# A gated delta-rule attention and mixture-of-experts layer: each expert's earliest tokens kept as running lists through attention, and five of eight shared groups placed behind the experts

## The chip, the cores and the metric

The kernel runs on one core of a Trainium2 chip. Its engines are TensorE (PE), VectorE (DVE), ScalarE (ACT), GpSimd (POOL) and SyncE (SP), each with an instruction queue of its own that runs in order. The metric is the device time of one execution in microseconds (us). The profile is of one execution; the times before are three other ones.

## The reference, cut to what matters

```python
B, S, D = 2, 2048, 256; H, DK, DV = 16, 128, 128; SEG = 64      # attention
def step(carry, seg):                     # 32 segments in order, per head and batch
    mem, z = carry; qq, kk, vv = seg
    att_dot = softmax(where(causal, qq @ kk.T / scale, -inf)) @ vv
    att_mem = sigma_q @ mem / (sigma_q @ z)
    delta = vv - sigma_k @ mem / (sigma_k @ z)
    mem_new = mem + sigma_k.T @ delta
    z_new = z + sigma_k.sum(tokens)
    att = beta * att_mem + (1 - beta) * att_dot
    return (mem_new, z_new), att @ Wo
x1 = x + attention(layernorm(x)); h = layernorm(x1)

E, K, G, TG, CAP = 32, 4, 4, 2, 64        # experts, 4 of 32 per token
topk_idx, topk_w = gate(h)                # sigmoid, best 2 of 4 groups, best 4 experts
pos = cumsum(one_hot(topk_idx)) - 1       # place of a token in its expert's queue
keep = pos < CAP                          # an expert takes its 64 earliest tokens
out = sum_k topk_w[k] * expert(topk_idx[k], h) where keep
shared = silu(h @ shared_gate) * (h @ shared_up) @ shared_down
return x1 + out + shared
```

Of the 4096 tokens (2 batches of 2048) each expert keeps only the 64 that come first, so all but the earliest picks of an expert are dropped.

## The kernel before

**Attention.** The program walks over 16 blocks of 128 tokens (of both batches at once), and in each block over 8 pairs of heads, the steps g = 0 to 7 (`body(blk, first, last)`, written once for every engine and unrolled). Step n = 8 blk + g has two segments (seg 0 and 1). TensorE's row of work in a step: numerators of segment 0 (L1354), projections for the next step (L1305), update of segment 0 (L1364), numerators of segment 1, projections, update of segment 1, `attend` (L1381), scores of the next step (L1328), then the numerators of the next step. `numerators` waits for the semaphore `mem_ready`, which VectorE's `state(n, g, seg)` gives after it has subtracted the update from the memory (two instructions at L902, of `chain_k` and `chain_q`). VectorE's row in a step ends: delta of segment 1 (L883 to L892), whatever of the layer norms and the gate stands in that step, `sigma_q(n + 1)` (L868), `state(n, g, 1)` (L902), and then the next step's `attended` (L911), mask (L1074) and maximum (L1079).

The rest of the layer rides along one block late: output projection in g = 0 (`project_out`, L1410), residual in g = 1 (L919), layer norm in g = 1 to 3, gate in g = 5 to 7. GpSimd does the elementwise work between (L474, L480, L489, L498).

**Routing.** `picks(blk)` (L1007) turns a block's picks into one descending number for each token (`N` minus its place; 0 if not picked), 32 experts on 32 partitions by 256 tokens, and SyncE writes it to the DRAM tensor `picks`. After the last block GpSimd writes that block's part itself, reads the whole tensor back as `vq` (128 partitions, four quarters of the tokens, by 1024), and `top8` (L1056 MAX8, L1057 MATCH_REPLACE8) takes the eight greatest eight times over; the four lists of 64 are moved side by side (`cm`, 32 x 256) and `top8` runs eight times again. The result gives the token numbers for the gathers of GpSimd (L573).

**Shared expert.** 8 groups (`NTG`) of 2 blocks. A group is `shared_up` (two halves fc, each a gate and an up product, L1462), ScalarE's silu (L744), VectorE's `shared_mul` (L1044), `shared_down` (L1481) and `shared_add` into `acc` (L1050). `shared_mul(g, fc)` waits until `shared_down(g - 1)` is over, since both use the buffer `sh`. `FRONT = 7` groups stand ahead of the experts, one behind them. The first half of group 0 stands inside the last attention step, where there is nothing to project, and waits there for the shared weights to land.

**Experts.** 16 pairs (`NP`): gather rows, transpose (`columns`, L1498), up (L1510), down (L1526), merge (L1538 to L1541), and GpSimd scatters the rows with an accumulate to the DRAM tensor `y` (L586). When all 16 scatters have landed, SyncE loads `y` in four parts (L431), VectorE adds each to `acc` (`sum_add`, L1276) and SyncE stores it (L436).

## Time and profile before

| | us |
|---|---|
| median of three executions | 1823.45 (1822.89 to 1825.72) |
| the profiled execution: its time | 1825.59 |
| the profiled execution: its span, first to last instruction | 1823.7 |
| TensorE busy in the span | 1728.6 (95%), 17990 matmuls |
| VectorE busy | 1208.0 (66%) |
| ScalarE, GpSimd busy | 805.4 (44%), 916.7 (50%) |

The profiled execution's time is 1.9 us over its span and 2.1 us over the median. A busy share is a mean over very different stages: the attention loop fills nearly 1640 us of the span, the rest of the layer the last 184 us. In rows of the timeline the columns are start, duration, engine, line, operation, written and read tiles, shapes and count, and in square brackets the idle time of the engine before it with what ended it.

### The profile page before, as it was taken

The numbers are of one execution on the slowest core, as the hardware profiler recorded it, in microseconds if no ns is written. First come the engines' busy times: TensorE is split into PE (matmuls) and PEld (weight loads), VectorE is DVE, ScalarE is ACT, GpSimd is POOL, SyncE is SP. The second block draws the span as 40 slices with busy tenths as digits, with TensorE's granted clock in tenths as the row PEclk, the third lists the DMA queues.
The fourth block names the chain that finished last, engine by engine and source line by source line (L and its number), as shares of the span: only waits on it lengthen the run. The fifth ranks groups of instructions, "written<-read, shape, count | busy, mean of one in ns | idle before, by whom it ended". The sixth has DMA issues, their size and how long they took to land. (4 is left out here: it accounts for less than half of the span.)

```text
span 1823.7 us, 45885 instructions
## 1 busy us (share of the span) xinstructions
PE 1728.6 (95%) x17990; PEld 1473.8 (81%) x17990; DVE 1208.0 (66%) x3996; ACT 805.4 (44%) x1936; POOL 916.7 (50%) x830
## 2 busy tenths in 40 slices
PE   6999999999999999999999999999999999989893
PEld 5788888888888888888888888888888888866451
DVE  6766757575767767575767677675767675663852
ACT  3544535353535445353535354453535354541040
POOL 3655646464646546464646455454646464530162
PEclk8999999999999999999999999999999999999997
DMA  4200000100000000001000000000010000046747
GB/s 152 70 22 25 15 19 8 32 8 25 15 15 25 15 25 15 19 8 32 8 22 18 15 25 15 25 15 19 8 32 8 15 25 9 25 148 188 207 80 202
DMA packets 83190, 75.23 MB, mean 41 GB/s; under 512 B 20992, under 2 KB 73808, under 8 KB 82720
## 3 DMA queue, kind: packets, MB, share of 16 engines
q1 hardware_dynamic: 79264, 65.89, 11.9%
q0 software_dynamic: 3680, 6.40, 1.9%
q8 instruction: 144, 2.36, 0.5%
q14 instruction: 70, 0.57, 0.1%
q10 hardware_dynamic: 32, 0.01, 0.0%
HBM read 47.78 MB, written 24.47 MB: 40 GB/s over the span
## 5 line engine op out<-in xcount | busy, mean ns | idle before, releaser
L489 POOL TENSOR_TENSOR step_place<-step_place 128x512 f32<-128x512 f32 x128 | 169.7, 1326 | 243.5 <-ACT step_place L645 243.5
L659 ACT ACTIVATE step_place<-chain_q,step_place 128x128 f32<-128x128 f32 x512 | 159.9, 366 | 275.2 <-DVE step_place L886 274.9
L902 DVE TENSOR_TENSOR step_place<-step_place,chain_k 128x258 f32<-128x258 f32 x256 | 107.7, 421 | 260.7 <-PE chain_q L1364 260.6
L525 POOL TENSOR_TENSOR step_place<-step_place 128x256 f32<-128x256 f32 x128 | 78.8, 615 | 313.5 <-DVE step_place L1079 313.5
L1410 PE MATMUL bank_o<-step_place 128*128 128x256 f32 x1024 | 226.0, 379 | 0.0
L480 POOL TENSOR_SCALAR step_place<-step_place 128x512 f32<-128x512 f32 x128 | 191.0, 1492 | 44.0 <-ACT step_place L639 43.9
L1410 PEld LDWEIGHTS bank_o<-step_place 128*128 128x128 f32 x1024 | 192.3, 190 | 25.4 <-issue 0.5
L474 POOL TENSOR_SCALAR step_place<-step_place 128x512 f32<-128x512 f32 x128 | 190.3, 1486 | 0.3 <-POOL step_place L498 0.3
L1354 PE MATMUL chain_k<-step_place 128*64 128x129 f32 x2048 | 166.0, 282 | 20.3 <-DVE step_place L902 20.2
L1364 PE MATMUL chain_k<-step_place 64*128 64x129 f32 x1024 | 181.4, 297 | 1.8 <-ACT step_place L659 1.1
L1364 PE MATMUL chain_q<-step_place 64*128 64x129 f32 x1024 | 181.6, 297 | 0.0
L1364 PEld LDWEIGHTS chain_k<-step_place 64*128 64x128 f32 x1024 | 132.4, 186 | 44.8 <-issue 42.3
L498 POOL TENSOR_TENSOR step_place<-step_place 128x512 f32<-128x512 f32 x128 | 164.6, 1286 | 0.0
L892 DVE SCALAR_TENSOR_TENSOR step_place<-chain_k,step_place 128x128 f32<-128x128 f32 x512 | 154.4, 342 | 6.1 <-DVE step_place L883 0.8
L1354 PE MATMUL chain_q<-step_place 128*64 128x129 f32 x2048 | 158.1, 273 | 0.0
L532 POOL TENSOR_TENSOR step_place<-step_place 128x256 f32<-128x256 f32 x128 | 78.5, 613 | 153.6 <-DVE step_place L1087 153.6
L652 ACT ACTIVATE step_place<-bank_k 128x512 f32<-128x512 f32 x128 | 76.7, 599 | 160.4 <-PE chain_q L1364 155.6
L1354 PEld LDWEIGHTS chain_k<-step_place 128*64 128x64 f32 x2048 | 109.2, 137 | 43.2 <-issue 29.3
L627 ACT ACTIVATE step_place<-bank_q 128x512 f32<-128x512 f32 x128 | 76.5, 598 | 136.0 <-PE bank_q L1305 136.0
L1364 PEld LDWEIGHTS chain_q<-step_place 64*128 64x128 f32 x1024 | 132.5, 186 | 0.0
L1354 PEld LDWEIGHTS chain_q<-step_place 128*64 128x64 f32 x2048 | 122.8, 136 | 0.0
L1305 PE MATMUL bank_k<-xt_hi,w_hi 128*128 128x256 f32 x512 | 116.6, 309 | 1.1 <-DVE xt_lo L860 1.1
(201 smaller groups left out, 4342.1 us busy)
## 6 DMA issues: line engine op xcount, KB each, us to landing
expert_place<-in_L_ffn_w_dram SPq DMA_DIRECT2D x24, 512.0 KB, 7.8
expert_sums<-zero SPq DMA_DIRECT2D x16, 272.0 KB, 5.1
expert_rows<-w_in SPq DMA_DIRECT2D x15, 288.0 KB, 2.2
step_place<-in_L_attn_x_dram SPq DMA_DIRECT2D x16, 256.0 KB, 3.0
x_res<-in_L_attn_x_dram SPq DMA_DIRECT2D x16, 256.0 KB, 3.2
x_rows<-w_in SPq DMA_DIRECT2D x16, 256.0 KB, 2.0
x_normed_t<-x1t SPq DMA_DIRECT2D x16, 256.0 KB, 2.0
shared_place<-x_normed_t SPq DMA_DIRECT2D x8, 512.0 KB, 8.2
```

The source lines that it names most:

```text
L474: nc.gpsimd.tensor_scalar(ex_q[:, :], ex_q[:, :], 1.0, None, ALU.min).then_inc(s["q_min"], 1)
L480: nc.gpsimd.tensor_scalar(ex_k[:, :], ex_k[:, :], 1.0, None, ALU.min).then_inc(s["k_min"], 1)
L489: nc.gpsimd.tensor_tensor(vb[:, :, :, :].rearrange("p s j d -> p s (j d)"), val[:, :, :, :].rearrange("p s j d -> p s (j d)"), rows.unsque ...
L498: nc.gpsimd.tensor_tensor(vo[:, :, :, :], val[:, :, :, :], vb[:, :, :, :], ALU.subtract).then_inc(s["vo_ready"], 1)
L525: nc.gpsimd.tensor_tensor(sm[:, :, :], sm[:, :, :], smx[:, :].unsqueeze(2).to_broadcast([128, T, SEG]), ALU.subtract).then_inc(s["s_shifte ...
L659: ins = nc.scalar.activation(am[:, par, seg, j, :], chain_q[:, j * ZC:j * ZC + DK], ACT.Copy, scale=rdq[:, seg, j:j + 1])
L892: ins = nc.vector.scalar_tensor_tensor(out=dl[seg][:, j, 0:DK], in0=chain_k[:, j * ZC:j * ZC + DK], scalar=rdk[:, seg, j:j + 1], in1=vb[:, ...
L902: ins = nc.vector.tensor_tensor(m, m, (chain_k, chain_q)[b][:, 0:HG * ZC].rearrange("p (j z) -> p j z", j=HG), ALU.subtract)
L1305: ins = mm(out, w[:, g, m, c, col], x[:, c, :, :].rearrange("p s t -> p (s t)"), start=i == 0, stop=i == len(parts) - 1)
L1354: ins = mm(out[ROWS[half], j * ZC:(j + 1) * ZC], sig[:, j, seg, b, :], mem[:, HG * g + j, b, :], start=True, stop=True)
L1364: ins = mm((chain_k, chain_q)[b][:, j * ZC:(j + 1) * ZC], ksig[ROWS[b], j, seg, :], dl[seg][ROWS[b], j, :], start=True, stop=True)
L1410: ins = mm(bank_o[:, b * D:(b + 1) * D], att[:, b * PIECES + i, :], wo[:, i, :], start=(i == 0 and b == 0), stop=(i == PIECES - 1), skip_g ...
```

## The change

- The lists of the earliest tokens are kept while attention runs. A buffer `earliest[blk % 2]` has one partition for each batch and expert (64), with 64 places for the list so far and 128 for the block's new picks. `picks` writes the 128 new numbers, and in every step g of blocks 2 to 15 one round (`earliest_of`: a MAX8 and a MATCH_REPLACE8 over 64 x 192) stands between `sigma_q` and `state`. The last block's eight rounds stand behind the loop. The DRAM tensor `picks`, `vq`, `cm` and their transfers are gone; after the last gate 8 rounds run over 32 x 384.
- `FRONT = 3`: three shared groups stand ahead of the experts and five behind. The half of group 0 that stood in the last step goes behind the last output projection.
- The loads of `x1t` for groups 4 to 7 wait until the scatters have left their places. The four `sum_add` stand between the shared groups behind the experts, and the last two blocks are stored one by one.

```diff
-STEP_PLACE = 23808
+STEP_PLACE = 23760
-    FRONT = 7
+    FRONT = 3
-    XSLOT = [0, 1, 2, 3, 4, 0, 1, 4]
+    XSLOT = [0, 1, 2, 4, 0, 1, 2, 3]
...
+        for g in range(4, NTG):
+            sp.wait_ge(s2["added"], 64 * (g - 3))
+            load_columns(g)
...
-        for k in range(NK):
+        for k in range(NK - 1):
             sp.wait_ge(s2["y_added"], k + 1)
             store(k * YB, (k + 1) * YB)
+        sp.wait_ge(s2["y_added"], NK)
+        store((NK - 1) * YB, NBLK - TG)
+        for k in range(NBLK - TG, NBLK):
+            sp.wait_ge(s2["acc_ready"], k + 1)
+            store(k, k + 1)
...
-        for q in range(QUARTERS):
-            pool.dma_start(vq[q * E:(q + 1) * E, :], scratch["picks"][:, q * QUART:(q + 1) * QUART]
-                           ).then_inc(s2["vq_arrived"], 16)
...
         def picks(blk):
...
+            nc.vector.tensor_tensor(earliest[blk % 2][:, CAP:CAP + BLK], bank_o[0:B * E, 0:BLK],
+                                    desc[:, :], ALU.mult).then_inc(s["pickv_ready"], 1)
             dve.wait_ge(s["pickv_ready"], blk + 1)
+            nc.vector.tensor_scalar_add(desc[:, :], desc[:, :], -float(BLK)
                                         ).then_inc(s["desc_ready"], 1)
+        def earliest_of(blk, r):
+
+            link = link_on(dve, s["list_step"], 2 * ROUNDS * (blk - 1) + 2 * r + 1)
+            have, kept = earliest[blk % 2], earliest[(blk + 1) % 2][:, 8 * r:8 * r + 8]
+            link(nc.vector.max(kept, have[:, :]))
+            link(nc.vector.match_replace(out=have[:, :], in_to_replace=kept, in_values=have[:, :],
+                                         imm_value=-1.0))
...
                     sigma_q(n + 1, (g + 1) % 2)
+                if blk > 1:
+                    earliest_of(blk - 1, g)
                 if first and g + 2 < NG:
                     split_lo(g + 2)
                 state(n, g, 1)
...
+        for r in range(ROUNDS):
+            earliest_of(NBLK - 1, r)
...
         for r in range(ROUNDS):
+            top8(sel, pool_last[:, :, :].rearrange("p b c -> p (b c)"), r)
+            if r == 0:
+                shared_mul(1, 0)
+            if r == 2:
+                shared_mul(1, 1)
+            if r in (3, 4):
+                shared_add(0, r - 3)
+            if r == 6:
+                shared_mul(2, 0)
...
+        for g in range(FRONT, NTG):
+            shared_mul(g, 0)
+            if g > FRONT:
+                for k in range(TG):
+                    shared_add(g - 1, k)
+            if g == NTG - 2:
+                sum_add(0)
+            if g == NTG - 1:
+                sum_add(2)
+            shared_mul(g, 1)
+            if g == NTG - 2:
+                sum_add(1)
+            if g == NTG - 1:
+                sum_add(3)
+        dve.wait_ge(s2["y_added"], NK)
```

The instructions that move, as they stand in the two programs. First VectorE, step g = 1 of the last block, from the statistics of the residual to the next step's first addition. Before:

```order
L818 BN_STATS st_x<-w_in 128x6 x2
L821 BN_AGGR mv_x<-st_x 128x2 x2
L823 TENSOR_SCALAR v_x<-mv_x 128x2
L824 TENSOR_SCALAR a_x<-v_x 128x2
L826 TENSOR_SCALAR rs_x<-a_x 128x2
L868 SCALAR_TENSOR_TENSOR step_place<-bank_q,step_place 128x512
L902 TENSOR_TENSOR step_place<-step_place,chain_k 128x2x129
L902 TENSOR_TENSOR step_place<-step_place,chain_q 128x2x129
L911 TENSOR_TENSOR step_place<-step_place,bank_a 128x256
```

After:

```order
L807 TENSOR_SCALAR v_x<-mv_x 128x2
L808 TENSOR_SCALAR a_x<-v_x 128x2
L810 TENSOR_SCALAR rs_x<-a_x 128x2
L852 SCALAR_TENSOR_TENSOR step_place<-bank_q,step_place 128x512
L1006 MAX earliest<-w_in 64x8
L1007 MATCH_REPLACE w_in<-earliest,w_in 64x192
L886 TENSOR_TENSOR step_place<-step_place,chain_k 128x2x129
L886 TENSOR_TENSOR step_place<-step_place,chain_q 128x2x129
L895 TENSOR_TENSOR step_place<-step_place,bank_a 128x256
```

A round of the list now stands in the queue between `sigma_q` and `state`. Next TensorE, from the last `attend` (L1381, after L1382) to the rows behind the last output projection (L1410, after L1411). Before:

```order
L1381 MATMUL bank_a<-step_place 64x128 x2
L1381 MATMUL bank_v<-step_place 64x128 x2
L1462 MATMUL chain_k<-shared_place 128x512 x2
L1391 MATMUL bank_a<-step_place 128x2x16x4 x4
L1462 MATMUL chain_q<-shared_place 128x512 x2
L1410 MATMUL bank_o<-step_place 128x256 x32
```

After:

```order
L1382 MATMUL bank_a<-step_place 64x128 x2
L1382 MATMUL bank_v<-step_place 64x128 x2
L1392 MATMUL bank_a<-step_place 128x2x16x4 x4
L1411 MATMUL bank_o<-step_place 128x256 x32
L1461 MATMUL bank_q<-shared_place 128x512 x2
L1461 MATMUL bank_k<-shared_place 128x512 x2
L1461 MATMUL chain_k<-shared_place 128x512 x2
L1421 MATMUL bank_o<-ident,w_in 128x128 x4
L1429 MATMUL bank_o<-gwt,x1t 128x32 x4
```

No shared product is left ahead of the output projection, and none between the transposes of the normed rows and the logits. Last, the end of TensorE's program. Before, from the last merge on:

```order
L1538 MATMUL chain_q<-shared_place 128x256
L1539 MATMUL chain_q<-shared_place 128x256
L1541 MATMUL bank_s<-shared_place 128x256
L1462 MATMUL bank_q<-shared_place 128x512 x2
L1462 MATMUL bank_k<-shared_place 128x512 x2
L1462 MATMUL chain_k<-shared_place 128x512 x2
L1462 MATMUL chain_q<-shared_place 128x512 x2
L1481 MATMUL bank_s<-shared_place 128x256 x4
L1481 MATMUL bank_v<-shared_place 128x256 x4
```

After, the last two groups of the five:

```order
L1461 MATMUL chain_k<-shared_place 128x512 x2
L1461 MATMUL chain_q<-shared_place 128x512 x2
L1461 MATMUL bank_q<-shared_place 128x512 x2
L1461 MATMUL bank_k<-shared_place 128x512 x2
L1480 MATMUL bank_s<-shared_place 128x256 x4
L1480 MATMUL bank_v<-shared_place 128x256 x4
L1461 MATMUL chain_k<-shared_place 128x512 x2
L1461 MATMUL chain_q<-shared_place 128x512 x2
L1480 MATMUL bank_s<-shared_place 128x256 x4
L1480 MATMUL bank_v<-shared_place 128x256 x4
```

A group's down product stands between the two halves of the next group's up product, and the last one stands alone.

## Rows read from the trace of the kernel before

**Rows 1.** Timeline, VectorE and TensorE at the ends of block 14's steps 0 to 3

```profile
1452.18 0.42 DVE L902 TENSOR_TENSOR step_place<-step_place,chain_k 128x258 f32<-128x258 f32 x1 [7.92 <-PE chain_q L1364]
...
1462.65 0.41 DVE L902 TENSOR_TENSOR step_place<-step_place,chain_k 128x258 f32<-128x258 f32 x1
...
1472.94 0.42 DVE L902 TENSOR_TENSOR step_place<-step_place,chain_k 128x258 f32<-128x258 f32 x1 [0.32 <-PE chain_q L1364]
1473.28 0.42 DVE L902 TENSOR_TENSOR step_place<-step_place,chain_q 128x258 f32<-128x258 f32 x1
...
1473.94 0.61 PE L1354 MATMUL chain_k<-step_place 128*64 128x129 f32 x8
...
1483.74 0.42 DVE L902 TENSOR_TENSOR step_place<-step_place,chain_k 128x258 f32<-128x258 f32 x1 [0.74 <-PE chain_q L1364]
```

**Rows 2.** Timeline, the same two engines at the ends of steps 5 to 7

```profile
1505.63 0.42 DVE L902 TENSOR_TENSOR step_place<-step_place,chain_k 128x258 f32<-128x258 f32 x1 [0.44 <-PE chain_q L1364]
...
1516.91 0.42 DVE L902 TENSOR_TENSOR step_place<-step_place,chain_q 128x258 f32<-128x258 f32 x1
...
1517.76 0.61 PE L1354 MATMUL chain_k<-step_place 128*64 128x129 f32 x8
...
1529.01 0.40 DVE L902 TENSOR_TENSOR step_place<-step_place,chain_q 128x258 f32<-128x258 f32 x1
...
1529.56 0.66 PE L1354 MATMUL chain_k<-step_place 128*64 128x129 f32 x8 [1.07 <-DVE step_place L902]
```

**Rows 3.** Timeline, VectorE: starts of two neighbouring rounds, of 1024 and of 256

```profile
1686.00 1.23 DVE L1056 MAX8 shared_place<-shared_place 128x8 f32<-128x1024 f32 x1 [8.21 <-DMA shared_place<-picks]
...
1688.58 1.23 DVE L1056 MAX8 shared_place<-shared_place 128x8 f32<-128x1024 f32 x1
...
1719.08 0.42 DVE L1056 MAX8 shared_place<-shared_place 32x8 f32<-32x256 f32 x1
...
1720.04 0.42 DVE L1056 MAX8 shared_place<-shared_place 32x8 f32<-32x256 f32 x1
```

**Rows 4.** Timeline, VectorE in step 6 of block 14, while GpSimd is busy

```profile
1511.77 0.15 DVE L963 MATCH_REPLACE8 grp<-glist,gsx 128x10 f32<-128x10 f32 x1
...
1512.09 1.28 DVE L966 TENSOR_SCALAR gm<-grp 128x8 f32<-128x8 f32 x1
```

**Rows 5.** Timeline, TensorE from the last step to the last output projection

```profile
1623.57 3.75 PE L1462 MATMUL bank_q<-shared_place 128*128 128x512 f32 x4 [3.37 <-DMA shared_place<-x_normed_t]
...
1630.29 0.37 PE L1364 MATMUL chain_k<-step_place 64*128 64x129 f32 x1
...
1640.36 13.98 PE L1410 MATMUL bank_o<-step_place 128*128 128x256 f32 x64
```

**Rows 6.** Timeline, VectorE: residual of the last block; the multiply behind its picks

```profile
1654.38 0.69 DVE L919 TENSOR_TENSOR w_in<-bank_o,x_res 128x512 f32<-128x512 f32 x1 [13.05 <-PE bank_o L1410]
...
1670.86 0.66 DVE L1044 TENSOR_TENSOR shared_place<-shared_place,chain_q 128x512 f32<-128x512 f32 x1
```

**Rows 7.** Timeline, TensorE: down products two groups apart, first expert columns, shared group behind

```profile
1701.67 1.89 PE L1481 MATMUL bank_v<-shared_place 128*128 128x256 f32 x8
...
1722.31 1.89 PE L1481 MATMUL bank_v<-shared_place 128*128 128x256 f32 x8
...
1733.01 0.38 PE L1498 MATMUL bank_o<-ident,shared_place 128*128 128x128 f32 x2
...
1782.74 1.98 PE L1462 MATMUL bank_q<-shared_place 128*128 128x512 f32 x4 [0.47 <-ACT shared_place L786]
```

**Rows 8.** DMA issues: count, KB each, median us from issue to landing

```profile
x_rows<-w_in SPq DMA_DIRECT2D x16, 256.0 KB, 2.0
...
shared_place<-picks POOLq DMA_DIRECT2D x4, 128.0 KB, 6.7
...
shared_place<-expert_rows,shared_place POOLq DMA_INDIRECT x16, 3.0
```

**Rows 9.** Busy time in a stretch; the number behind POOL is the granted clock

```profile
1620.00:1640.00 20.00, 14.25 (x80) 7.57 (x77) 7.57 (x31) 5.94 (x15) 2.45 (x3) 0.83 0.76 266
```

More of the change, by code:

```diff
@@ L216, in layer @@
     wsum = sb("wsum", [128, 3, B])
[L217 removed]
+    desc = sb("desc", [B * E, BLK])
     small = sil[:, :, :].rearrange("p a c -> p (a c)")
@@ L412, in _ @@
         sp.wait_ge(s["wo_mm"], NBLK)
-        for i in range(NB // 2):
-            load_batch(i)
-        sp.wait_ge(s2["u_mm"], 2 * FC)
-        load_columns(6)
-        for i in range(NB // 2, NB):
+        for i in range(NB):
             load_batch(i)
@@ L466, in _ @@
                                     channel_multiplier=1).then_inc(s["const_ready"], 1)
-        nc.gpsimd.iota(desc[:, :, :], pattern=[[-S, B], [-1, BLK]], base=N, channel_multiplier=0,
-                       allow_small_or_imprecise_dtypes=True).then_inc(s["desc_ready"], 1)
+        pool.wait_ge(s["const_ready"], 3)
+        for b in range(B):
+            nc.gpsimd.iota(desc[b * E:(b + 1) * E, :], pattern=[[-1, BLK]], base=N - b * S,
+                           channel_multiplier=0, allow_small_or_imprecise_dtypes=True
+                           ).then_inc(s["desc_ready"], 1)
         def cap_queries(n):
@@ L754, in _ @@
         ins.then_inc(s2["ident_kept"], 1)
-        shared_silu(1, 0)
+        shared_silu(0, 0)
+        shared_silu(0, 1)
         side_x1t(NBLK)
         logits_exp(NBLK)
-        shared_silu(1, 1)
-        for g in range(2, FRONT):
+        for g in range(1, FRONT):
             for fc in range(FC):
@@ L1135, in _ @@
         attended(NT - 1, (NG - 1) % 2)
-        for fc in range(FC):
-            shared_mul(0, fc)
+        for r in range(ROUNDS):
+            earliest_of(NBLK - 1, r)
+        for b in range(B):
+            ins = nc.vector.tensor_copy(pool_last[:, b, 0:CAP],
+                                        earliest[NBLK % 2][b * E:(b + 1) * E, 0:CAP])
+        ins.then_inc(s["lists_kept"], 1)
         residual(NBLK)
@@ L1141, in _ @@
         x1_apply(NBLK)
-        dve.wait_ge(acc_arrived[0], 16)
-        for k in range(TG):
-            shared_add(0, k)
-        shared_mul(1, 0)
+        shared_mul(0, 0)
         gate_scores(NBLK)
@@ L1190, in _ @@
         for k in range(TG):
-            shared_add(5, k)
-        for fc in range(FC):
-            shared_mul(6, fc)
+            shared_add(1, k)
+        shared_mul(2, 1)
         def weights(q):
@@ L1276, in sum_add @@
             nc.vector.tensor_tensor(a, a, y, ALU.add).then_inc(s2["y_added"], 1)
-        for fc in range(FC):
-            shared_mul(NTG - 1, fc)
+        for g in range(FRONT, NTG):
[13 more added lines that the diff above has]
+        dve.wait_ge(s2["y_added"], NK)
         for k in range(TG):
             shared_add(NTG - 1, k)
-        for k in range(NK):
-            sum_add(k)
     @block.tensor
@@ L1433, in pick_transposes @@
             pe.wait_ge(s["gate_step"], GATE_STEPS * (blk - 1) + PICK_STEP)
-            for b in range(B):
-                ins = nc.tensor.transpose(bank_o[0:E, b * BLK:(b + 1) * BLK], pick[:, b, :],
-                                          ident[:, :])
-            ins.then_inc(s["pickt_mm"], 1)
+            nc.tensor.transpose(bank_o[0:B * E, 0:BLK], pick[:, :, :].rearrange("p b e -> p (b e)"),
+                                ident[:, :]).then_inc(s["pickt_mm"], 1)
         pe.wait_ge(s["ident_ready"], 6)
@@ L1599, in _ @@
         pe.wait_ge(s["mem_ready"], 2 * NT)
-        shared_half(0, 1, 0)
         attended_transposes(NT - 1, (NG - 1) % 2)
-        shared_half(0, 1, 1)
         pe.wait_ge(s["pickv_ready"], NBLK)
         project_out(0, PIECES, NT)
-        shared_down(0)
-        pe.wait_ge(xt_arrived[1], 16)
-        shared_half(1, 0, 0)
-        x1_transposes(NBLK)
-        shared_half(1, 0, 1)
-        logits(NBLK)
-        shared_up(1, 1)
+        pe.wait_ge(s2["shared_arrived"], 48)
+        shared_up(0, 0)
+        shared_half(0, 1, 0)
+        x1_transposes(NBLK)
+        logits(NBLK)
+        shared_half(0, 1, 1)
+        shared_up(1, 0)
+        pick_transposes(NBLK)
+        shared_up(1, 1)
+        shared_down(0)
         shared_up(2, 0)
-        pick_transposes(NBLK)
-        shared_half(2, 1, 0)
         shared_down(1)
-        shared_half(2, 1, 1)
-        for g in range(3, FRONT):
-            shared_up(g, 0)
-            shared_down(g - 1)
-            if g == FRONT - 1:
-                pe.wait_ge(s["pickv_ready"], NBLK + 1)
-                pair_tokens()
-            shared_up(g, 1)
-        shared_down(FRONT - 1)
+        pe.wait_ge(s["pickv_ready"], NBLK + 1)
+        pair_tokens()
+        shared_up(2, 1)
+        shared_down(2)
         columns(0)
@@ L1638, in _ @@
         pe.wait_ge(s2["yo_ready"], NP)
-        shared_up(NTG - 1, 0)
-        shared_up(NTG - 1, 1)
+        for g in range(FRONT, NTG):
+            shared_up(g, 0)
+            if g > FRONT:
+                shared_down(g - 1)
+            shared_up(g, 1)
         shared_down(NTG - 1)
```

108 lines of the change are left out of this document (33 added, 75 removed).

## The prediction

> **What bounds the kernel now.** I read the timeline first, at the ends of the steps of one attention block, because the change puts two VectorE instructions into every one of them. Attention is a loop of 100.6 us per block (step 0 of block 14 ends its wait at 1452.18 [rows 1]; the pattern repeats to 0.1 us in blocks 2 to 14). TensorE is nearly gapless there, so anything that makes it wait is paid in full, 14 times. The question at each step's end is who comes last: VectorE with `state` (L902), which TensorE's next numerators (L1354) wait for, or TensorE with its own queue. The bracket behind an L902 row is VectorE's idle time, that is, its cover. In step 0 it is 7.92 us, in step 1 none, in step 2 0.32, in step 3 0.74 [rows 1], in step 5 0.44, in steps 6 and 7 none [rows 2]. There is a second, smaller cover: the time from the end of `state` to TensorE's start. Where TensorE really waits (step 7, bracket 1.07) it is 1529.56 - 1529.41 = 0.15 [rows 2]. In step 2 it is 1473.94 - 1473.70 = 0.24 [rows 1], so 0.09 is slack; in step 6 it is 1517.76 - 1517.33 = 0.43 [rows 2], so 0.28 is slack.
>
> Then the timeline behind the loop. TensorE waits 3.37 us for the shared weights and does a shared half before it can go on with the last step [rows 5]. Later VectorE waits 8.21 us for `picks` to come back from DRAM [rows 3], and then makes lists for 38 us, while shared groups fill TensorE. At the end only scatters, loads of `y`, adds and stores are left.
>
> **Part 1: a list round in each step.** The trace has no round of 192, but two sizes beside it, with their waits in the start-to-start time: 2.58 us for 1024 (1686.00 to 1688.58) and 0.96 for 256 (1719.08 to 1720.04) [rows 3]. The slope is 1.62 / 768 = 0.0021 us per element, so 192 takes 0.96 - 64 x 0.0021 = 0.83 us. Bounds: not over 0.96, the row of 256, and not under some 0.55, which the fixed part would be if the line were steeper near its foot. I take 0.83, from the nearest row. GpSimd is busy beside it, and some VectorE instructions wait for it: a TENSOR_SCALAR of 8 elements takes 1.28 us, while a MATCH_REPLACE8 just before it takes 0.15 [rows 4]. So the match form does not wait, and I add nothing. The Trainium skill, SBUF — State Buffer, Who interferes with whom, says that a VectorE instruction with at most one SBUF input outside the two-port modes does not contend with GpSimd; by that rule, the trace agrees.
>
> What of 0.83 reaches TensorE, step by step: step 0 nothing; step 1 0.83; step 2 0.83 - 0.32 - 0.09 = 0.42; steps 3 and 4 nothing (0.74 idle and more slack; step 4 has more idle time still); step 5 0.83 - 0.44 - 0.09 = 0.30; step 6 0.83 - 0.28 = 0.55; step 7 0.83, since there VectorE is last already. A delay is not made up later, since TensorE has no idle time to give back, and it does not grow, since VectorE waits for TensorE in the middle of each step. Sum 2.93, or 5x - 1.22 for a round of x. For 13 blocks 38.0 us. In the last block (steps 1, 2, 5 and 6, the last without slack) 4x - 0.94 = 2.4. Together **+40 us**. The cheaper picks (64 x 128 in place of 32 x 256, one transpose fewer) are worth perhaps 0.1 us a block, in step 7 alone; I leave them out. The eight rounds behind the loop (6.6 us) lie under the output projection, 13.98 us [rows 5], for which VectorE only waits (13.05) [rows 6]. Without that cover they would cost their 6.6.
>
> **Part 2: the end of attention.** TensorE has its numerators done at 1623.57 - 3.37 = 1620.20 and starts the update at 1630.29 [rows 5]. With no load to wait for, the update needs only VectorE's delta, some 1.0 us: 9.1 us gained. VectorE takes back about 0.9 of it on the way to the last `attended` (a round, and its softmax sum comes last). Ahead of the output projection at 1640.36 [rows 5] two shared halves of 1.7 us go, and about 1.4 us of waits for VectorE and ScalarE that they covered stay open: 2.0 gained. Together **-10.2 us**.
>
> **Part 3: from the residual to the experts.** Before: 1654.38 [rows 6] to 1733.01 [rows 7], 78.6 us. A group costs TensorE half of 1722.31 - 1701.67, 10.3 us [rows 7], and four of them leave this stretch, but what bounds it then is VectorE's chain. Counted from the residual: the multiply behind the picks ended at 17.1 (1670.86 + 0.66 [rows 6]); logits come 0.6 earlier and the picks are 0.5 shorter, so 16.0. A round of 384 takes 0.96 + 128 x 0.0021 = 1.23. The first ends at 17.2. Then `shared_mul(1, 0)` stands in VectorE's queue, and it waits for `shared_down(0)`, which TensorE can begin only when the multiply at 16.0 has let it finish the second half of group 1 (17.7) and ends 3.45 later, at 21.1. Seven rounds (8.6) and five VectorE shared operations at 0.6 lead to 32.8, the three index steps, the transposes and the copies to 34.2. TensorE has run dry meanwhile, and then does the second half of group 2 (3.4), waits for its multiply (0.9) and does the down product (3.45): the first expert columns stand at 41.8. So **-36.8 us**.
>
> The gathers now start while the expert weights are still streaming: SyncE starts them 7 us behind the residual and needs over 40 us, as before. Small transfers of GpSimd took 3.0 us to land behind that stream (gathers) and 6.7 in the midst of it (`picks`) [rows 8]. The first gather would land at 35.3 + 6.7 = 42.0, just in time. But gathers 2 and on are queued on GpSimd behind the wait for the token list's store, and VectorE's second `hidden` behind the 1 MB token load. I put **+4 us** on it, between 0 (all lands in 3.0) and 9 (nothing lands before the weights are through).
>
> **Part 4: the end.** Before, the experts give way to the last group at 1782.74 [rows 7] and the span ends at 1823.7. Scatters, loads and adds of `y` (some 30 us) are now covered by five groups: 1782.74 + 5 x 10.3 = 1834.3; about 1.5 for the last multiply, which stands behind an add of `y`; 0.7 for the last add; 0.9 to issue two stores and 2.0 to land (a store of 256 KB [rows 8]): 1839.4, **+15.7 us**. If the `y` loads were late, they would have 20 us to spare.
>
> **Part 5: the clock.** Between 1620 and 1640 TensorE had 0.83 of its clock [rows 9]: 0.17 x 20 / 0.5 = 6.8 us at 1.2 in place of 2.4 GHz, after short stops and the one of 3.37. After the change two stretches are as thin: the last step, and the wait for the index. A fall costs up to half its length where TensorE is busy, so 0 to 3.4 each: **+2 us**.
>
> **Sum.** 40.4 - 10.2 - 36.8 + 4 + 15.7 + 2 = +15.1. Span 1823.7 + 15.1 = 1838.8; the profiled execution was 1.9 over its span and 2.1 over the median, so the forecast is **1838.5 us**, 0.8% slower. The tail gains 25 us and the loop loses 40.
>
> **Rivals.** (a) *The round is cheap or finds cover: faster.* Place: between L868 and L902 in steps 1, 2, 5, 6, 7. The loop costs 69x - 16.8 in all. It breaks even with the tail at 25 us, x = 0.61, and the kernel is over 0.2% faster under x = 0.56. At x = 0.4 the time would be 1811 (the terms of steps 2 and 5 end at nothing). For it: the MATCH_REPLACE8 of 10 elements takes 0.15 [rows 4], so the fixed part is small. Against it: the two sizes of rows 3 lie on one line, and 192 is close to 256. (b) *Partly covered*: a time of 1820 to 1827, if steps 2, 5 and 6 give more slack than their rows (that is 17 us of the 40). (c) *The longer stops pull down the clock.* The stop in step 7 grows from 1.07 [rows 2] to 1.9 us. The clock stayed at 2.4 GHz through all stops of 1.07, and fell after the thin stretch with the one of 3.37 [rows 5, 9]. If it falls in a third of the blocks, at 2 to 3.4 us each, that is 8 to 15 us: 1847 to 1854. The Trainium skill, TensorE: Matmul & The Clock Gate, HAM oscillation, tells of loops that throttle in every pass because of stops in them; by that rule it could be all 14 blocks, near 1880. (d) *The experts do not start early*, since their gathers and the token list land only with the last weights: 5 us more, 1844, and with two cold stretches 1848.
>
> **How the numbers follow.** Forecast 0.60 (own range 1829 to 1846), (a) 0.12, (b) 0.08, (c) 0.14, (d) 0.06. A measurement of this kernel can tell about 0.2%, 3.6 us, from no change. Slower by more: 0.80; within: 0.08; faster: 0.12. The range of 1822 to 1852 leaves out (a) and the upper part of (c).
>
> **What would show it.** In the trace after: MAX8 and MATCH_REPLACE8 of 64 x 192, 0.83 us from start to start of their neighbours; a block period of 103.5 us in place of 100.6; waits of TensorE for L902's successor in steps 1, 2, 5, 6 of 0.8, 0.4, 0.3, 0.5 us and 1.9 in step 7; output projection to first columns 37 us shorter; TensorE busy to some 4 us before the end. A period under 102.4 with the tail as computed would make the prediction wrong in sign, and a granted clock under 0.98 between the second and fourteenth block would make it (c).

## The result, and the profile of the changed kernel

The changed kernel takes 1857.22 us (median of four executions, 1855.78 to 1858.58) against 1823.69 of the kernel before beside it: ratio 1.0182, 95% interval 1.0164 to 1.0200. The forecast was 1838.5 us with a range of 1822 to 1852. The direction was right, the loss is 33.5 us in place of 15, and the time lies outside the range. The profiled execution of the changed kernel took 1855.78 us with a span of 1854.0.

Where the 30.3 us of span went, from the same marks in both traces (in us; a negative number is a gain):

| stretch | before | after | difference | forecast |
|---|---|---|---|---|
| start to step 0 of block 2 | 221.7 | 222.25 | +0.6 | 0 |
| blocks 2 to 14 | 1307.9 | 1355.6 | +47.8 | +38.0 |
| block 15, its steps 0 to 6 | 89.5 | 93.8 | +4.3 | +2.4 |
| last step to last output projection | 21.26 | 12.01 | -9.25 | -10.2 |
| projection to residual | 14.02 | 15.82 | +1.8 | 0 |
| residual to first expert columns | 78.63 | 43.90 | -34.7 | -36.8 |
| columns to the first group behind the experts | 49.73 | 53.40 | +3.7 | +4 |
| from there to the end | 40.96 | 57.2 | +16.2 | +15.7 |

The clock's +2 of the forecast belongs to the last five lines together. These came to -22.3 where -25.3 was forecast; the first three came to +52.6 where +40.4 was forecast.

First the marks and waits of TensorE. The timeline's columns are those of the groups of before. Kernel before, TensorE, the two marks not shown yet (step 0 of block 2, last step of block 15):

```profile
221.70 0.55 PE L1354 MATMUL chain_k<-step_place 128*64 128x129 f32 x6 [1.08 <-DVE step_place L902]
...
1619.10 0.66 PE L1354 MATMUL chain_k<-step_place 128*64 128x129 f32 x8 [1.37 <-DVE step_place L902]
```

Changed kernel, TensorE's numerators (L1355): the mark at block 2, behind steps 1, 6 and 7 of block 3, behind step 7 of block 4, and the mark at block 15. They answer to the TensorE rows of [rows 1, 2]:

```profile
222.25 0.55 PE L1355 MATMUL chain_k<-step_place 128*64 128x129 f32 x6 [1.33 <-DVE step_place L886]
...
361.22 0.33 PE L1355 MATMUL chain_k<-step_place 128*64 128x129 f32 x2 [0.67 <-DVE step_place L886]
...
416.72 0.44 PE L1355 MATMUL chain_k<-step_place 128*64 128x129 f32 x4 [0.37 <-DVE step_place L886]
...
429.40 0.33 PE L1355 MATMUL chain_k<-step_place 128*64 128x129 f32 x2 [2.00 <-DVE step_place L886]
...
532.93 0.66 PE L1355 MATMUL chain_k<-step_place 128*64 128x129 f32 x8 [2.01 <-DVE step_place L886]
...
1577.89 0.66 PE L1355 MATMUL chain_k<-step_place 128*64 128x129 f32 x4 [2.52 <-DVE step_place L886]
```

The cause of the waits stands on VectorE, between `sigma_q` (L852) and `state` (L886), at the end of block 4:

```profile
530.61 0.67 DVE L852 SCALAR_TENSOR_TENSOR step_place<-bank_q,step_place 128x512 f32<-128x512 f32 x1
531.21 0.34 DVE L1006 MAX8 w_in<-earliest 64x8 f32<-64x192 f32 x1
531.58 0.08 DVE L1007 MATCH_VALUE_LOAD earliest<-w_in,earliest 64x8 f32 x1
531.66 0.33 DVE L1007 MATCH_REPLACE8 earliest<-w_in,earliest 64x192 f32<-64x192 f32 x1
532.03 0.42 DVE L886 TENSOR_TENSOR step_place<-step_place,chain_k 128x258 f32<-128x258 f32 x1
```

A round costs 532.03 - 531.21 = 0.82 us, as forecast, and the block period without anything else is 103.5 to 103.6, as forecast. Every second block or so is longer. Busy time in stretches of the changed kernel (the number behind POOL's is the clock granted to TensorE as a share of 2.4 GHz): blocks 4 and 5, then the 3.4 us around the stop that ends block 4 and the 3.4 us behind it:

```profile
429.40:532.90 103.50, 99.70 (x1089) 87.32 (x1089) 74.59 (x261) 47.40 (x115) 53.65 (x48) 1.00 0.06 17
532.90:638.00 105.10, 101.25 (x1090) 88.76 (x1090) 74.68 (x261) 47.36 (x115) 53.61 (x48) 0.98 0.06 17
...
530.10:533.50 3.40, 1.39 (x34) 1.15 (x28) 3.33 (x10) 0.31 (x1) 0.51 (x1) 1.00 0.55 164
533.50:536.90 3.40, 3.40 (x22) 3.06 (x18) 2.16 (x8) 0.93 (x3) 1.17 (x2) 0.50 0.03 7
```

Behind the stop of 2.01 us TensorE has 1.2 GHz for 3.4 us; step 0 of block 5 takes 25.72 us in place of 24.22, so the fall costs 1.5 us. The trace has seven of these falls, at the starts of blocks 5, 6, 8, 10, 11, 13 and 15 (the last behind the stop of 2.52 us): 10.5 us. The kernel before had none between 41.8 and 1622.

Now the part behind the loop. Changed kernel, TensorE:

```profile
1671.69 0.66 PE L1355 MATMUL chain_k<-step_place 128*64 128x129 f32 x8 [2.56 <-DVE step_place L886]
...
1683.70 15.78 PE L1411 MATMUL bank_o<-step_place 128*128 128x256 f32 x64 [0.90 <-ACT step_place L660]
...
1726.73 1.96 PE L1480 MATMUL bank_s<-shared_place 128*128 128x256 f32 x8 [2.41 <-DVE shared_place L1046]
...
1733.41 0.29 PE L1487 MATMUL bank_o<-ident,shared_place 32*64 32x16 f32 x4 [2.96 <-DVE shared_place L1176]
1733.63 2.48 PE L1461 MATMUL chain_k<-shared_place 128*128 128x512 f32 x4
1735.90 3.13 PE L1461 MATMUL chain_q<-shared_place 128*128 128x512 f32 x4
...
1743.42 0.38 PE L1497 MATMUL bank_o<-ident,shared_place 128*128 128x128 f32 x2
...
1748.64 0.69 PE L1497 MATMUL bank_o<-ident,shared_place 128*128 128x128 f32 x2 [2.79 <-DMA shared_place<-expert_rows,shared_place]
...
1796.82 1.98 PE L1461 MATMUL bank_q<-shared_place 128*128 128x512 f32 x4 [0.47 <-ACT shared_place L770]
```

and VectorE: the residual, the multiply of group 1 between the rounds over 384 places, the index:

```profile
1699.52 0.69 DVE L903 TENSOR_TENSOR w_in<-bank_o,x_res 128x512 f32<-128x512 f32 x1 [10.99 <-PE bank_o L1411]
...
1721.02 0.69 DVE L1040 TENSOR_TENSOR shared_place<-shared_place,bank_k 128x512 f32<-128x512 f32 x1 [4.53 <-PE bank_v L1480]
...
1733.81 0.17 DVE L1178 CAST shared_place<-bank_o 128x16 uint32<-128x16 f32 x1 [0.54 <-PE bank_o L1487]
```

The output projection is stretched from 13.98 us [rows 5] to 15.78, and the two matmul groups at 1733.63 and 1735.90 take 2.48 and 3.13 us where their neighbours take 1.88: the granted clock was at 1.2 GHz from 1680.4 to 1687.2 and from 1735.0 to 1738.4.

### The profile page after: what moved, and what is told of

It is laid out like the page before. It is cut to its first block, busy times and chain, and to the rows that moved or that the text cites. A ratio compares the mean times of both kernels' runs of the same rounds, so it can differ in the third digit from the quotient of the medians.

```text
span 1854.0 us, 46269 instructions
## 1 busy us (share of the span) xinstructions
PE 1750.4 (94%) x17974; PEld 1488.9 (80%) x17974; DVE 1269.1 (68%) x4335; ACT 804.5 (43%) x1936; POOL 912.5 (49%) x822
## 4 chain that ended last, share of the span: by engine, by line
PE 69%; DVE 21%; issue 4%; ACT 2%; POOL 2%; DMA 1%; SPq 0%; DVEq 0%; POOLq 0%; ACTq 0%
PE bank_o L1411 12%; PE bank_k L1306 10%; PE bank_q L1306 9%; PE chain_k L1355 7%; PE chain_k L1365 5%; PE chain_q L1355 5%; PE bank_v L1316 5%; PE bank_a L1392 3%; DVE step_place L886 3%; PE bank_s L1329 2%; DVE step_place L852 2%; PE bank_a L1382 2%; DVE step_place L876 2%; PE bank_s L1400 1%; PE bank_k L1338 1%
## 5 line engine op out<-in xcount | busy, mean ns | idle before, releaser
L886 DVE TENSOR_TENSOR step_place<-step_place,chain_k 128x258 f32<-128x258 f32 x256 | 108.4, 423 | 223.0 <-PE chain_q L1365 218.7
L1411 PE MATMUL bank_o<-step_place 128*128 128x256 f32 x1024 | 227.8, 381 | 0.9 <-ACT step_place L660 0.9
L1355 PE MATMUL chain_k<-step_place 128*64 128x129 f32 x2048 | 169.2, 284 | 51.2 <-DVE step_place L886 50.7
L1411 PEld LDWEIGHTS bank_o<-step_place 128*128 128x128 f32 x1024 | 193.5, 191 | 26.6 <-issue 1.3
L1355 PEld LDWEIGHTS chain_k<-step_place 128*64 128x64 f32 x2048 | 111.1, 137 | 80.3 <-issue 65.0
L1355 PE MATMUL chain_q<-step_place 128*64 128x129 f32 x2048 | 161.5, 275 | 0.0
L1355 PEld LDWEIGHTS chain_q<-step_place 128*64 128x64 f32 x2048 | 125.7, 137 | 0.0
```

The costliest lines, as they stand in the source:

```text
L886: ins = nc.vector.tensor_tensor(m, m, (chain_k, chain_q)[b][:, 0:HG * ZC].rearrange("p (j z) -> p j z", j=HG), ALU.subtract)
L1355: ins = mm(out[ROWS[half], j * ZC:(j + 1) * ZC], sig[:, j, seg, b, :], mem[:, HG * g + j, b, :], start=True, stop=True)
L1411: ins = mm(bank_o[:, b * D:(b + 1) * D], att[:, b * PIECES + i, :], wo[:, i, :], start=(i == 0 and b == 0), stop=(i == PIECES - 1), skip_g ...
```

## Experiments

The loop costs more than its rounds by the clock, in the profile of one execution. The theory: **one long stop** of TensorE, at the end of step 7, brings the clock down. The rivals: the sum of the stops in a block does it, or something else of the change (its transfers, its picks). The first four kernels move rounds between step 0, where VectorE has 7.92 us of idle time [rows 1], and the others. All their edits are the same line with another condition:

```diff
                 if blk > 1:
-                    earliest_of(blk - 1, g)
+                    for r in range(ROUNDS):
+                        if 0 == g:
+                            earliest_of(blk - 1, r)
```

with `(7 if r > 6 else 0) == g` for one round in step 7, `(7 if r > 5 else 0) == g` for two, and `max(r - 1, 0) == g` for none in step 7.

### All rounds in step 0

> The changed kernel with all eight rounds of a block's list in step 0, where VectorE had 7.9 us of idle time before the second state; eight rounds take 8 x 0.82 = 6.6 us. If the rounds cost only what TensorE waits for, and the falls of the clock come only from the longer stop at the end of step 7 (2.0 us in place of 1.07), then the block period goes back from 103.55 to 100.6 us and no fall is left between the second and the last block: span 1854.0 - 38.4 (13 blocks) - 3.2 (last two) - 10.5 (seven falls of 1.5) = 1802, time about 1804. That is then the change's tail alone, 22 us under the kernel before. If the falls have another cause in the changed kernel (its new DMA traffic, its smaller picks), they stay: about 1814. If step 0 has less cover than its idle time says (the round's instructions wait for something there), the period ends between 101 and 103 us: 1808 to 1835.

Measured: 1801.92 us, 1.2% under the kernel before (ratio 0.9880, 0.9864 to 0.9897). The block period is 100.57 us and no fall is left in the loop. VectorE in step 0 of block 3, the end of the last round and the `state` that follows, and the stretch of the loop:

```profile
343.50 0.33 DVE L1007 MATCH_REPLACE8 w_in<-earliest,w_in 64x192 f32<-64x192 f32 x1
345.29 0.42 DVE L886 TENSOR_TENSOR step_place<-step_place,chain_k 128x258 f32<-128x258 f32 x1 [1.45 <-PE chain_q L1367]
```

```profile
42.00:1620.00 1578.00, 1546.18 (x17089) 1359.26 (x17088) 1161.42 (x3977) 752.04 (x1813) 849.73 (x755) 1.00 0.07 20
```

After eight rounds VectorE still waits 1.45 us for TensorE. The 112 rounds of the loop, with which (falls included) the changed kernel's loop took 52 us more, cost nothing here, and the falls went with the stops. This kernel is the change without the loop's cost: the rest of it is worth 22.7 us in the medians.

### One round in step 7

> Seven rounds in step 0 (covered), the eighth in step 7 as in the changed kernel. The only stop that grows is the one at the end of step 7, to 2.0 us; those of steps 1, 2, 5 and 6 are gone. Theory 'the single long stop': the clock still falls behind it in about half of the blocks: period 101.5 without a fall, loop +13 us and 7 falls at 1.5 us, 1804 + 13 + 10.5 = 1827. Rival 'the sum of the stops in a block' (3.2 us in the changed kernel, 2.0 here): no or hardly any fall, 1817.

Measured: 1828.60 us (ratio 1.0023, 1.0013 to 1.0033). Blocks 2 and 3:

```profile
222.40:323.90 101.50, 98.91 (x1091) 87.03 (x1092) 75.21 (x261) 47.49 (x115) 53.65 (x48) 1.00 0.06 18
323.90:426.80 102.90, 100.35 (x1089) 88.27 (x1090) 74.09 (x261) 47.49 (x115) 53.67 (x48) 0.98 0.06 18
```

Nine of the thirteen stops of 1.97 us were followed by a fall, each 1.5 us, in blocks 3 to 6, 8, 9, 11, 13 and 14. The sum of the stops in a block is 2.0 us, less than the 3.2 of the changed kernel, and the falls are not fewer. That speaks against the rival of the sum, and no round in steps 1 to 6 is needed for a fall.

### Two rounds in step 7

> Six rounds in step 0, two in step 7: the stop there grows to 2.0 + 0.82 = 2.8 us. Theory 'the single long stop', graded by its length: the clock falls behind nearly every one of the 14 stops, loop +24.5 us and 14 falls at 1.5 us: 1804 + 24.5 + 21 = 1850. Rival 'the length does not matter over some 2 us, only where in time the stop lies': about half of the blocks, 1804 + 24.5 + 10.5 = 1839.

Measured: 1839.99 us (ratio 1.0088, 1.0071 to 1.0105). Blocks 3 and 4:

```profile
323.80:428.80 105.00, 101.56 (x1091) 89.33 (x1092) 74.14 (x261) 47.36 (x115) 53.68 (x48) 0.97 0.06 17
428.80:532.50 103.70, 100.35 (x1089) 88.25 (x1089) 75.05 (x261) 47.45 (x115) 53.65 (x48) 0.98 0.06 17
```

Here my theory failed in its graded form. Six of thirteen stops of 2.80 us brought a fall, not all; three of the six lasted 6.8 us (blocks 3, 7 and 12) and cost 2.6, the others (4, 8 and 13) 3.4 us and 1.5. The three long falls began 0.9 to 1.1 us before the end of the stop, the three short ones at most 0.2 us before it. A longer stop made some falls longer, not more of them. The time is that of the rival, by which it matters where in time the stop lies.

### None in step 7

> Two rounds in step 0, one each in steps 1 to 6, none in step 7: the stops of steps 1, 2, 5 and 6 stay as in the changed kernel (0.67, 0.16, 0.04, 0.37 us), and that of step 7 goes back to about 1.2; the sum of the stops in a block is 2.4 us, more than the 2.0 of the kernel with one round in step 7. Theory 'the single long stop': no fall between the second and the last block, period 102.7: 1857 - 12.5 - 10.5 = 1834. Rival 'the sum of the stops': falls in a third to half of the blocks, 1840 to 1845.

Measured: 1835.77 us (ratio 1.0054, 1.0038 to 1.0071). The loop up to its last step, and the 20 us from that step's start on:

```profile
42.00:1650.00 1608.00, 1557.25 (x17082) 1364.49 (x17083) 1153.18 (x3976) 750.73 (x1814) 849.16 (x756) 1.00 0.07 20
1650.00:1670.00 20.00, 16.13 (x91) 12.29 (x87) 13.81 (x57) 4.95 (x13) 2.45 (x3) 0.57 0.73 268
```

No fall from 42 to 1650 us, with stops of 0.67, 0.16, 0.04, 0.36 and 1.16 us in every block: 2.4 us of stops in many pieces leave the clock alone, and 2.0 in one piece do not. That settles it between the two theories. The period of 102.7 and the time are as expected. Two stops of TensorE in this kernel are longer, ahead of block 15 and of the last step:

```profile
1557.45 0.66 PE L1357 MATMUL chain_k<-step_place 128*64 128x129 f32 x8 [1.67 <-DVE step_place L886]
...
1649.35 0.66 PE L1357 MATMUL chain_k<-step_place 128*64 128x129 f32 x8 [2.20 <-DVE step_place L886]
```

No fall followed the first. Behind the second, 1.3 us after its end, the clock fell for 17 us, through the rest of the last step and into the output projection.

### A stop half way

Against the kernel with all rounds in step 0; the new argument says which of the round's two instructions are given out, 0 for MAX8 and 1 for MATCH_REPLACE8:

```diff
-                            earliest_of(blk - 1, r)
+                            earliest_of(blk - 1, r, (0, 1) if r else (1,))
+                if 0 < blk < NBLK - 1 and g == NG - 1:
+                    earliest_of(blk, 0, (0,))
```

> All rounds in step 0, except that the first MAX8 of the next block's list (0.38 us) already stands in step 7 behind the picks, its MATCH_REPLACE8 in step 0. The stop at the end of step 7 becomes 1.12 + 0.38 = 1.5 us, half way between 1.12 (no fall in 13 blocks) and 1.97 (nine falls). Period 100.57 + 0.38 = 100.95, loop +5.3 us over the kernel with all in step 0. Theory 'a stop has to be long': no fall, 1801.9 + 5.3 = 1807. Rival 'every lengthening brings some falls': three to five of them at 1.5 us, 1812 to 1815.

Measured: 1810.23 us (ratio 0.9920, 0.9903 to 0.9936). Blocks 2 and 3, and the stops ahead of them:

```profile
221.90:324.40 102.50, 100.39 (x1091) 88.32 (x1092) 74.15 (x261) 47.44 (x115) 53.61 (x48) 0.98 0.06 17
324.40:425.30 100.90, 98.83 (x1089) 86.89 (x1089) 75.07 (x261) 47.45 (x115) 53.60 (x48) 1.00 0.06 18
```

```profile
221.87 0.55 PE L1362 MATMUL chain_k<-step_place 128*64 128x129 f32 x6 [1.72 <-DVE step_place L886]
...
324.37 0.44 PE L1362 MATMUL chain_k<-step_place 128*64 128x129 f32 x4 [1.52 <-DVE step_place L886]
```

Thirteen stops of 1.52 us were followed by no fall; the one stop of 1.72 was. The time lies between the two expectations (1807, and 1812 to 1815). One fall behind the stop of 1.72, and none behind that of 1.67 in the kernel before this one, do not fix a length at which falls begin.

### Three rounds in step 1

The condition is `(1 if r > 4 else 0) == g`.

> Five rounds in step 0, three in step 1: the long stop now stands at the end of step 1, 0.67 + 2 x 0.82 = 2.3 us, and that of step 7 is back at 1.12. Period 100.57 + 2.45 = 103.0, so the loop costs 14 x 2.45 = 34 us over the kernel with all in step 0. Theory 'any single stop of some 2 us can bring the clock down, wherever it is': falls behind the end of step 1 in four to ten blocks at 1.5 us, 1836 + 6 to 15 = 1842 to 1851. Rival 'only at a block's end, where the stop comes together with the thin rows of small products around the picks and the next numerators': no fall, 1836.

Measured: 1847.02 us (ratio 1.0120, 1.0103 to 1.0137). TensorE behind step 1 of block 2, and blocks 2 and 3:

```profile
259.48 0.66 PE L1357 MATMUL chain_k<-step_place 128*64 128x129 f32 x8 [2.33 <-DVE step_place L886]
```

```profile
222.40:327.00 104.60, 100.56 (x1089) 88.47 (x1090) 75.19 (x261) 47.47 (x115) 53.66 (x48) 0.98 0.06 17
327.00:430.10 103.10, 99.03 (x1089) 87.00 (x1090) 75.15 (x261) 47.50 (x115) 53.65 (x48) 1.00 0.06 17
```

Six falls behind fourteen stops, in blocks 2, 4, 7, 10, 13 and 15. A long stop brings falls away from a block's end too, so the small products there are not what it takes. The regular distance, two or three blocks, speaks for the stop's place in time again, but is not shown to be the cause.

All kernels together, from one profiled execution each. A fall is counted when the clock goes down close to the end of the stop (at most 1.2 us before it or 1.6 us behind it). The stops ahead of the very last step are left out: of the two long ones, that of 2.20 us above was followed by a fall, and that of 2.56 us in the changed kernel was not for 8.7 us.

| stop, us | where | stops | falls |
|---|---|---|---|
| 1.07 | kernel before, step 7 | 14 | 0 |
| 1.12 | all in step 0, step 7 | 13 | 0 |
| 1.16 | none in step 7, step 7 | 12 | 0 |
| 1.52 | half way, step 7 | 13 | 0 |
| 1.67 | none in step 7, ahead of block 15 | 1 | 0 |
| 1.72 | half way, ahead of block 2 | 1 | 1 |
| 1.97 | one in step 7 | 13 | 9 |
| 2.00 | changed kernel, step 7 | 12 | 6 |
| 2.33 | three in step 1 | 14 | 6 |
| 2.52 | changed kernel, ahead of block 15 | 1 | 1 |
| 2.80 | two in step 7 | 13 | 6, three of them twice as long |

The counts can differ from one execution to the next: with one round in step 7 the granted clock over the whole span was 0.986 in the profiled execution and 0.983 to 0.987 in the others. So 9 of 13 against 6 of 12 or 6 of 14 does not show that one length brings more falls than another.

### The order behind the last gate

In the changed kernel VectorE waits 4.53 us for a down product in the middle of the rounds. With all rounds of the loop in step 0 and:

```diff
-            if r == 0:
+            if r == 3:
                 shared_mul(1, 0)
-            if r == 2:
                 shared_mul(1, 1)
-            if r in (3, 4):
-                shared_add(0, r - 3)
-            if r == 6:
-                shared_mul(2, 0)
+                shared_add(0, 0)
+                shared_add(0, 1)
...
+        shared_mul(2, 0)
         dve.wait_ge(s2["sel_mm"], 1)
```

> All rounds in step 0, and in the last part both multiplies of group 1 and the adds of group 0 behind the fourth round over 32 x 384 in place of behind the first and third; the multiply of group 2 behind the index steps. VectorE then makes three rounds more before it waits for the first down product: its wait falls from 4.53 us to about 0.7, the index is ready 3.8 to 4.5 us earlier, and TensorE's waits of 2.41 and 2.96 us in this stretch shrink. Residual to first expert columns 38 us in place of 42.4. If the experts can then start, 1798; if their gathered rows or the weights still arriving hold them, the gain comes back as waits of TensorE for the gathers behind pair 0, and the time stays within 1 us of 1801.9.

Measured: 1799.20 us (ratio 0.9861, 0.9845 to 0.9878). VectorE's wait, then TensorE at the first and third pair's columns:

```profile
1666.87 0.69 DVE L1040 TENSOR_TENSOR shared_place<-shared_place,bank_k 128x512 f32<-128x512 f32 x1 [0.85 <-PE bank_v L1480]
```

```profile
1683.30 0.38 PE L1497 MATMUL bank_o<-ident,shared_place 128*128 128x128 f32 x2
...
1689.60 0.69 PE L1497 MATMUL bank_o<-ident,shared_place 128*128 128x128 f32 x2 [3.87 <-DMA shared_place<-expert_rows,shared_place]
```

The wait fell to 0.85 us and the residual-to-columns stretch from 42.4 to 37.9, both as computed. In the profiled executions 0.55 us of these 4.5 came back between the first columns and the group behind the experts, where the wait for the third gather grew from 3.00 to 3.87. The medians lie 2.7 us apart, and the two intervals overlap, so the gain is shown by the stretches of one trace each and not by the times.

### Two gathers ahead of the token list

```diff
-        gather(0)
-        gather(1)
+        for p in range(4):
+            gather(p)
         pool.wait_ge(s2["toks_stored"], 16)
```

> As the kernel with the new order in the last part, and GpSimd issues the gathers of pairs 2 and 3 before it waits for the token list's store and issues the 1 MB token load. In the changed kernel TensorE waited 2.79 us for the gather of pair 2, which stood in the queue behind both. If that order is what delays it, TensorE's wait for the third gather goes and the time is 2 to 3 us under that of the new order alone. If it is the expert weights that still fill the queues, the gather lands as late as before and the time is the same; VectorE's second step for the experts, which waits for the token load, then comes 2 us later.

Measured: 1799.08 us (ratio 0.9861, 0.9845 to 0.9878), no difference. TensorE waits no more for the third gather, but now for VectorE, which waits for the token list:

```profile
1690.91 0.33 PE L1518 MATMUL chain_k<-ident,shared_place 128*128 128x128 f32 x1 [2.37 <-DVE shared_place L1198]
```

So the order in GpSimd's queue was what delayed the gather, the first half of what I expected. The gain did not follow, because the 1 MB token load is wanted at the same moment. Which of the two goes first makes no difference.

### Less in step 7

Step 7 is where VectorE comes last even in the kernel before. With the new order:

```diff
+
+        def numbers_on(blk):
             dve.wait_ge(s["pickv_ready"], blk + 1)
             nc.vector.tensor_scalar_add(desc[:, :], desc[:, :], -float(BLK)
                                         ).then_inc(s["desc_ready"], 1)
...
+                if blk > 1 and g == 0:
+                    numbers_on(blk - 1)
...
+        numbers_on(NBLK - 1)
```

The last line stands behind the loop.

> As the kernel with all rounds in step 0 and the new order in the last part; besides, the subtraction of 128 from the descending numbers (desc, a TENSOR_SCALAR of 64 x 128) leaves step 7, where VectorE comes last, and stands ahead of the rounds in step 0. In the changed kernel it took 0.79 us from start to start (0.86 busy, 0.22 where GpSimd does not hold it up). Theory: what VectorE does between the last delta and state in step 7 is what TensorE waits for, one for one; the stop shrinks from 1.12 to 0.33 us and the period from 100.57 to 99.8: 14 x 0.79 = 11 us less, 1788. Rival: the 0.64 us of it are a wait for GpSimd which then only moves to the next such instruction in step 7 (as it did in block 14 of the changed kernel, where an instruction of 0.39 took 1.41): 14 x 0.15 = 2 us less, 1797.

Measured: 1782.60 us, 2.3% under the kernel before (ratio 0.9773, 0.9760 to 0.9786). Kernel with all rounds in step 0, VectorE and then GpSimd at the end of block 4, and after the edit VectorE and TensorE at the same place:

```profile
520.39 0.28 DVE L996 TENSOR_TENSOR w_in<-bank_o,desc 64x128 f32<-64x128 f32 x1
520.70 1.04 DVE L999 TENSOR_SCALAR desc<-desc 64x128 f32<-64x128 f32 x1
521.67 0.67 DVE L852 SCALAR_TENSOR_TENSOR step_place<-bank_q,step_place 128x512 f32<-128x512 f32 x1
```

```profile
520.39 1.28 POOL L489 TENSOR_TENSOR step_place<-step_place 128x512 f32<-128x512 f32 x1 [0.69 <-ACT step_place L632]
```

```profile
516.95 0.28 DVE L996 TENSOR_TENSOR w_in<-bank_o,desc 64x128 f32<-64x128 f32 x1
517.16 0.67 DVE L852 SCALAR_TENSOR_TENSOR step_place<-bank_q,step_place 128x512 f32<-128x512 f32 x1
```

```profile
518.64 0.33 PE L1360 MATMUL chain_k<-step_place 128*64 128x129 f32 x2
```

The gain was 16.6 us, not 11. In this kernel the instruction was held until GpSimd's multiply ended at 521.67, so that its absence shortens the row from 1.28 us to 0.21 from start to start, and the stop from 1.12 to 0.04 us. The period is 99.5. The rival, that the wait moves to a neighbour, could hold at most in blocks 11 and 14, whose steps 7 are 0.3 and 0.2 us longer than the others'. The kernel before has the same wait in its step 7: there the subtraction started at 1527.18 and took 0.98 us, beside a multiply of GpSimd that ended at 1528.01. It is part of what made VectorE come last there, with TensorE's 1.07 us of idle time [rows 2].

A last edit puts `picks(blk)` of step 7 behind `state(n, g, 1)`.

> As the kernel with the numbers in step 0; besides, the multiply that writes the picks (0.32 us from start to start) stands behind state in step 7. The stop is then gone or nearly (0.33 - 0.32 = 0.01 us), period 99.5, 4 us less than with the numbers alone: 1784. Rival: state, then the multiply, then the next step's attended come 0.3 us later, and something that step 0 has no room for (the output projection waits for the picks) gives it back: no difference. Under both the clock has no reason to fall between the second and the last block.

Measured: 1781.59 us (ratio 0.9768, 0.9755 to 0.9781); the two intervals overlap. The period went from 99.47 to 99.30 us, less than expected only because the first edit had already taken nearly the whole stop.

## Why the prediction was right, and where it was wrong

**Part 1, the price of a round and its cover: right.** 0.82 us for 0.83; TensorE's waits 0.67, 0.16, 0.04, 0.37 and 2.0 us in steps 1, 2, 5, 6 and 7 for 0.8, 0.4, 0.3, 0.5 and 1.9; period 103.55 for 103.53. The steps grew by 0.84, 0.34, 0.25, 0.60 and 0.87 us (steps 1, 2, 5, 6, 7). The waits shown in steps 1, 2, 5 and 6 are some 0.2 us shorter than this growth: in the kernel before, the numerators' row begins up to 0.2 us ahead of the end of the scores' row, and that overlap goes first. That the cost is a matter of cover alone, and not of the rounds, the kernel with all in step 0 shows. The short term for the last block was 0.4 low, and block 14 took 0.5 more: the delay of 0.8 us puts other VectorE instructions beside GpSimd's. In step 7 of block 14 this one takes 1.41 us; in block 4 it took 0.39:

```profile
1573.66 1.41 DVE L981 TENSOR_SCALAR w_in<-wsel,wsum 128x32 f32<-128x32 f32 x2
```

I had asked only whether the new instruction waits for GpSimd, not which old ones it would push into GpSimd's way.

**The clock in the loop: the step that failed.** The sum put nothing for falls of the clock inside the loop. Part 1 computed the stop of 1.9 us and Part 5 counted falls only behind the loop; the falls in the loop stood as rival (c), with a chance of 0.14. They cost 10.5 us, within the 8 to 15 of that rival: seven of thirteen at 1.5, not a third at 2 to 3.4. This is over half of the miss; without them the time would have been 1846.7, inside the range. What the trace of before had to say was one stop length without a fall (1.07, fourteen times) and one with (3.37); a stop of 1.9 lies between, so "no fall" was no better founded than "a fall each time", and the sum should have carried half of it. The Trainium skill, TensorE: Matmul & The Clock Gate, HAM oscillation, tells of loops that throttle in every pass; the runs here bear out that a loop with stops can throttle again and again, but not every pass: 6 to 9 of 13 or 14 stops. My test for (c), a granted clock under 0.98 in the loop, was wrongly worked out as well: seven falls of 3.4 us at half clock leave 1 - 7 x 3.4 x 0.5 / 1630 = 0.993. A fall has to be looked for in its own few microseconds.

**Part 2: near.** -9.25 us for -10.2.

**Parts 3 and 5: the chain right, the clock low.** The index was ready 34.3 us behind the residual (1733.81 - 1699.52) where the working said 34.2. The first columns came at 43.9 in place of 41.8, and 1.85 of these 2.1 us are the two matmul groups at 1.2 GHz. With 1.8 in the output projection, and 0.9 in an expert group behind the fall at 1748.6 (1.98 us in place of 1.08), the clock took some 4.6 us behind the loop for the 2 of Part 5. The kernels with other loops show how little of it can be computed: the same stretch from projection to residual took from 15.7 to 17.0 us in them.

**The contention: right in kind, 2.8 us for 4.** The stretch grew by 3.7 us, but 0.9 of it is the fall at 1748.6 just named; the rest is TensorE's wait of 2.79 us for the third gather. That gather stands behind the token list, as the working said, and with two gathers moved ahead of the list the wait went. The gathers' median to landing rose to 6.2 us from 3.0 [rows 8]:

```profile
shared_place<-expert_rows,shared_place POOLq DMA_INDIRECT x16, 6.2
```

**Part 4: right.** +16.2 us for +15.7.

**Rivals (a), (b), (d).** (a) and (b) fell with the price of the round and the waits above; the tail's gain was real, 22.7 us in the kernel with all rounds in step 0. (d) did not happen.

**From the span to the median.** I put the median 0.3 us under the span, as for the kernel before. Here it is 3.2 over: 1.8 between span and time of the profiled execution, and 1.4 because that was the quickest of four. Together with the 0.3 that is 3.5 us of the miss. The whole miss of 18.7 is thus 10.5 of falls, 1.7 of the rest of the loop, 3.0 behind it and 3.5 here.

**What stays open:** why of two equal stops of 2.0 us one is followed by a fall and the other not, and at what length between 1.5 and 2.0 us falls begin. The counts above and the even distances with three rounds in step 1 point to where in time the stop lies; no run moved a stop by itself to test it.

## What to carry to other kernels

Put work that is needed later where its engine idles, not one piece into each step: the same rounds cost 52 us spread out, falls of the clock included, and nothing in the one step with cover, and then the next things to take away are whatever stands on the last engine's way in the step without cover. Where a change makes a recurring stop of TensorE longer than any that the trace shows without a fall of the clock, put a cost for falls in the sum, not in a side case. When instructions move, look again at all neighbours that share something with another engine, not only at the new ones.

## What the runs showed of the hardware that I had not expected

- Single stops of 1.97 to 2.80 us were followed by 3.4 us at 1.2 GHz in 28 of 53 cases, mostly at 1.5 us each, while 2.4 us of stops in five pieces per block, the longest 1.16, never were. Longer stops (2.80) did not bring more falls, but three of six lasted 6.8 us and cost 2.6.
- A subtraction on 64 x 128 numbers (0.22 us of work, as at other places) was busy 1.04 us beside a GpSimd multiply and ended with it; taking it off step 7 shortened each block by 1.1 us. MAX8 and MATCH_REPLACE8 of 64 x 192 took 0.34 and 0.33 us wherever they stood.
